# Mixed expert and attention network on one core: sums and low pieces taken out of the routing's way, the first tile's order, dummy products in PE's pauses, and a first attention batch prepared block by block

## The chip, the cores and the metric

The kernel runs on one core of one Trainium2 chip. The metric is the device time of one execution in microseconds. The engines are PE (TensorE), DVE (VectorE), ACT (ScalarE), POOL (GpSimd) and SP (SyncE, which here only issues transfers). Each works through its own queue in order, and they meet at semaphores.

## The reference, cut to what matters

```python
# x [8, 256, 512], cond [8, 512]
h  = gru(initial=cond, inputs=x)                    # 256 steps one after another
s  = einsum('bsd,ed->bse', h, w_gate_router)        # 8 experts
tv, ti = top_k(s, 2)
w  = sum(softmax(tv)[..., None] * one_hot(ti, 8), axis=-2)
hid = silu(gate_e(h)) * up_e(h)                     # 192 wide, per expert
x1 = x + einsum('bsef,edf,bse->bsd', hid, w_down, w)

scale, shift = split(cond @ W_emb + b_emb)
xn = rms_norm(x1, g_norm) * (1 + scale) + shift
q, k, v = split(xn @ W_qkv)                         # 16 heads of 32
q, k = rms_norm(q, g_q), rms_norm(k, g_k)
o  = softmax(q k^T / sqrt(32)) v
o2 = o + o @ W_out

t = lambda w: clip(round(w / (mean(abs(w)) + 1e-8)), -1, 1)
out = x1 + (sigmoid(o2 @ t(w1).T) * (o2 @ t(w2).T)) @ t(w3).T    # 1408 wide
```

## The kernel before

Everything is in one launch. Products are made in fp16 from a high part and a low part of each operand (`high_*` writes the high part, `low_*` the rest), three products for each exact one. Each stage is a list of calls per engine, written out by hand, and no scheduler changes the order. PE, DVE, ACT, POOL and SP each have a function in each of two blocks: the recurrence until about 825 us, and everything else.

The second block begins with the **routing**. For each of 16 groups of 128 tokens (`NG`), ACT and POOL split the states, PE multiplies them with the router and turns them (`route`), DVE sums the scores and takes the two largest (`sum_scores`, `top`, `top_index`), and ACT and DVE in turn copy the turned rows (`take_rows`), which SP saves to `hrows`. Between these stand pieces of weights: ACT makes their high part (`high_piece`), DVE their low part (`low_piece`), and SP loads the next piece into one of three buffers when the low part of the third before it is done. Pieces 8 to 15 are the experts' down weights, 16 to 19 those of q, k and v, 20 and 21 those of the output. Before its first sum DVE made the ternary thresholds and the adaptive scales (`thresholds`, `adapt`), which are used only much later.

Then come the **lists** that sort tokens by expert (`slots`, `owners`). DVE finds each token's slot, PE adds up ranks (`rank`), and 32 products of one-hot matrices (`rows_of_tiles`) give each tile of 128 slots its token rows. Their right side is `hot_row`: a one-hot tile number times the token's group offset. POOL then gathers the rows of each tile from `hrows` by indirect transfers into three buffers.

There are 39 **tiles** (`TILES`). For each, PE turns the rows (`turn_x`), DVE copies them (`take_x`), PE makes gate and up (`gate_up`), ACT and DVE the hidden values, PE turns these and multiplies them down, ACT scales the result, and POOL scatters it. `rest_of_tiles` gives the shares and is made once, beside the first tile.

**Attention** goes through eight batches of two blocks of 128 tokens. DVE or POOL add the two expert rows of a token (`first_sum`, `sum_rows`), DVE the residual; ACT makes the row norm (`square_rows`, `root_rows`, `unit_rows`), PE turns the rows (`turn_back`), and DVE (`adaptive`) or ACT (`turned`) apply scale and shift. PE makes six projections per batch (`project`: q and k of block 0, q and k of block 1, then v of each). Each q and k piece is copied, squared by POOL, summed, rooted, multiplied, split and stacked (`take_out`, `squares`, `sum_squares`, `root`, `invert`, `normalise_qk`, `high_qk`, `low_qk`, `stack`), and `scores` with `maximum` gives the row maxima of the 16 heads. In later batches this lies among the work of the batch before. For the first batch nothing else is there to do, and it stands by itself at the end of PE's, ACT's and DVE's functions: all of one step, then all of the next.

## Time and profile before

| | |
|---|---|
| Timed runs | 1696.36 us median of 3 (1693.38 to 1698.99) |
| Profiled execution | 1703.78 us, span 1702.0 us |
| Busy | PE 1552.9 us (91%), DVE 1187.9 (70%), ACT 900.0 (53%), POOL 609.9 (36%) |
| Recurrence | 0 to 825 us |
| Routing and lists | 825 to 869 us |
| 39 tiles | 869 to 1031.5 us |
| First batch prepared | 1038.7 to 1093.3 us |
| Eight batches and the ternary layers | to 1702 us |

Busy time is an average over stages with different limits, so each stage is read by itself. A row of the timeline gives the start, the duration, the engine and the line; the bracket at its end is how long the engine had been idle and what ended that. PEclk is the granted clock of PE as a part of 2.4 GHz. A duration of several merged instructions (x12) is the time from the first one's start to the last one's end.

### The profile page before, as it was taken

How to read it: one execution, taken by the hardware profiler on the slowest of the kernel's cores; microseconds unless marked ns; L12 is line 12 of the kernel's file. 1: busy time of each engine (PE TensorE's matmuls, PEld its weight loads, DVE VectorE, ACT ScalarE, POOL GpSimd, SP SyncE). 2: the span in 40 equal slices, each digit the busy share in tenths (PEclk: the TensorE clock that was granted, in tenths of full speed). 3: DMA queues.
4: the chain of work that ended last, by engine and by line, in shares of the span. 5: the costliest groups of instructions: out<-in, count | busy, mean ns of one | idle time of the engine just before them, and what ended most of it. 6: DMA issues, size and time to landing. Idle time of an engine off the chain costs nothing.

```text
span 1702.0 us, 76385 instructions
## 1 busy us (share of the span) xinstructions
PE 1552.9 (91%) x31935; PEld 1208.4 (71%) x31935; DVE 1187.9 (70%) x4289; ACT 900.0 (53%) x3329; POOL 609.9 (36%) x1819
## 2 busy tenths in 40 slices
PE   7999999999999999999759996778889888999999
PEld 6999999999999999999736553346556655544444
DVE  6778778787877778888865443677777777672231
ACT  6555555455555556655615444477777777531230
POOL 0333333333333333333625544344445443560000
PEclk9999999999999999955569997789999998999999
DMA  4110110101110011110435734000000010220001
GB/s 182 51 28 11 43 30 21 45 11 56 42 41 12 8 47 46 48 29 29 137 131 165 251 126 160 26 1 26 27 1 2 2 57 2 75 76 31 19 1 50
DMA packets 45735, 91.28 MB, mean 54 GB/s; under 512 B 6608, under 2 KB 25168, under 8 KB 45392
## 3 DMA queue, kind: packets, MB, share of 16 engines
q1 hardware_dynamic: 39152, 65.94, 12.0%
q0 software_dynamic: 6240, 20.45, 3.5%
q8 instruction: 254, 4.16, 1.0%
q14 instruction: 89, 0.73, 0.1%
HBM read 67.69 MB, written 18.61 MB: 51 GB/s over the span
## 4 chain that ended last, share of the span: by engine, by line
PE 29%; DVE 7%; ACT 7%; issue 3%; POOL 2%; DMA 1%; another core or an unknown queue 1%; SPq 0%; ACTq 0%; POOLq 0%; DVEq 0%
PE bank L1292 9%; PE bank L1178 5%; PE bank L1370 4%; PE bank L1102 3%; PE bank L1124 2%; ACT arena L1520 2%; POOL arena L2106 2%; ACT arena L1525 2%; PE bank L1196 1%; DVE arena L1917 1%; PE bank L1091 1%; PE bank L1249 1%; PE bank L1234 1%; PE bank L1273 1%
## 5 line engine op out<-in xcount | busy, mean ns | idle before, releaser
L412 PE MATMUL bank<-arena 128*128 128x8 f16 x12288 | 501.4, 170 | 9.2 <-issue 4.4
L415 PE MATMUL bank<-arena 128*128 128x16 f16 x12288 | 498.3, 182 | 3.4 <-issue 2.2
L412 PEld LDWEIGHTS bank<-arena 128*128 128x128 f16 x12288 | 412.7, 97 | 36.6 <-ACT bank L509 19.3
L415 PEld LDWEIGHTS bank<-arena 128*128 128x128 f16 x12288 | 412.8, 97 | 6.6 <-issue 5.0
L676 POOL TENSOR_TENSOR arena<-arena 128x16 f32<-128x16 f32 x512 | 116.8, 228 | 534.4 <-DVE arena L619 519.7
L479 ACT ACTIVATE arena<-arena 128x16 f32<-128x16 f32 x512 | 114.6, 224 | 308.6 <-DVE arena L598 308.3
L609 DVE TENSOR_TENSOR_SCAN arena<-arena,bank 128x64 f32<-128x64 f32 x512 | 146.8, 287 | 20.3 <-PE bank L415 3.1
L598 DVE TENSOR_REDUCE arena<-bank 128x16 f32<-128x48 f32 x512 | 100.2, 196 | 84.0 <-PE bank L415 78.7
L1292 PE MATMUL bank<-arena 128*128 128x512 f16 x704 | 153.6, 379 | 0.0
L385 PE MATMUL bank<-arena 128*128 128x256 f16 x1008 | 148.3, 273 | 2.6 <-issue 2.6
L1178 PE MATMUL bank<-arena 128*128 128x512 f16 x576 | 137.0, 389 | 4.0 <-DVE arena L1872 3.8
L615 DVE TENSOR_TENSOR_SCAN arena<-arena 128x48 f16<-128x48 f32 x512 | 134.1, 262 | 5.6 <-ACT arena L489 0.2
L489 ACT ACTIVATE arena<-arena 128x16 f32<-128x16 f32 x512 | 119.2, 233 | 24.1 <-DVE arena L609 6.1
L485 ACT ACTIVATE arena<-arena 128x16 f32<-128x16 f32 x512 | 110.3, 215 | 36.2 <-DVE arena L603 3.3
L1292 PEld LDWEIGHTS bank<-arena 128*128 128x128 f16 x704 | 68.9, 98 | 81.2
L603 DVE TENSOR_REDUCE arena<-bank 128x16 f32<-128x48 f32 x512 | 106.1, 207 | 27.1 <-PE bank L415 2.4
L2106 POOL TENSOR_TENSOR arena<-arena 128x512 f16<-128x512 f32 x56 | 67.7, 1210 | 147.3 <-ACT arena L1525 147.2
L677 POOL COPY arena<-arena 128x16 f32<-128x16 f32 x512 | 118.3, 231 | 0.0
L619 DVE TENSOR_TENSOR_SCAN arena<-arena 128x48 f32<-128x48 f32 x512 | 117.2, 229 | 0.4
L624 DVE TENSOR_TENSOR arena<-arena 128x16 f16<-128x16 f32 x512 | 95.8, 187 | 17.7
L1178 PEld LDWEIGHTS bank<-arena 128*128 128x128 f16 x576 | 56.8, 99 | 66.1 <-issue 5.6
L678 POOL COPY arena<-arena 128x16 f32<-128x16 f32 x512 | 102.6, 200 | 0.0
(209 smaller groups left out, 2676.8 us busy)
## 6 DMA issues: line engine op xcount, KB each, us to landing
arena<-yrows SPq DMA_DIRECT2D x16, 512.0 KB, 4.2
arena<-in_wgu SPq DMA_DIRECT2D x48, 128.0 KB
arena<-in_wdn SPq DMA_DIRECT2D x8, 512.0 KB
hrows<-arena SPq DMA_DIRECT2D x16, 256.0 KB, 4.5
arena<-in_xtok SPq DMA_DIRECT2D x16, 256.0 KB
out_y<-arena SPq DMA_DIRECT2D x16, 256.0 KB, 2.0
arena<-in_wih SPq DMA_DIRECT2D x4, 768.0 KB, 7.5
arena<-in_whh SPq DMA_DIRECT2D x4, 768.0 KB, 11.5
```

Of the source, the lines that this page charges most:

```text
L385: mm = nc.tensor.matmul(bank[7][:, half_of(mt)], wihs[:, wp, k, mt, :], xs[:, xp, k, half_of(c)], start=(i % 24 == 0), stop=(i % 12 == 11) ...
L412: mm = nc.tensor.matmul(dst[:, j * B:(j + 1) * B, 1], w, h[:, 0], start=home not in opened, stop=False, skip_group_check=True)
L415: mm = nc.tensor.matmul(dst[:, j * B:(j + 1) * B, 1:3], w, h.rearrange("p a c -> p c a"), start=home not in opened, stop=False, skip_group ...
L479: A.activation(fn[:, HALF[g], 3], rzp[:, 0, HALF[g]], ACT.Sigmoid, scale=1 / SWX).then_inc(r_act[g], 1)
L489: A.activation(inh[:, HALF[g], 0], sn[:, HALF[g], 3], ACT.Tanh, scale=1 / SWX).then_inc(n_act[g], 1)
L609: V.tensor_tensor_scan(flat(sn[:, HALF[g]]), flat(fn[:, HALF[g]]), flat(gate_sums(t, 2, g)), 0.0, ALU.mult, ALU.add).then_inc(n_pre[g], 1)
L615: V.tensor_tensor_scan(flat(mv[:, t % 2, 0, HALF[g]]), flat(fh[:, HALF[g]]), flat(inh[:, HALF[g]]), 0.0, ALU.mult, ALU.add).then_inc(h_hi[ ...
L619: V.tensor_tensor_scan(flat(sh[:, HALF[g]]), flat(fh[:, HALF[g]]), flat(inh[:, HALF[g]]), 0.0, ALU.mult, ALU.add).then_inc(h_f32[g], 1)
L676: G.tensor_tensor(inh[:, HALF[g], 1], zeros[:, :], sh[:, HALF[g], 2], ALU.subtract)
L677: G.tensor_copy(inh[:, HALF[g], 2], sh[:, HALF[g], 2])
L1178: mm = nc.tensor.matmul(bank[5 + i % 2][:, :], xn[:, x_, k, half * P:(half + 1) * P], wqs[:, w_, k, col:col + D], start=(n == 0), stop=(n ...
L1292: mm = nc.tensor.matmul(up_bank(a, u), w12[:, mt, a, k, :], o2p[:, 2 * c:2 * c + 2, part, k, :], start=(part == 0 and k == 0), stop=(part ...
```

## The change

It has five parts.

1. `thresholds` and `adapt` are divided. DVE reads their sums out of the banks where it did before (`sum_thresholds`, `take_adapt`); the rest follows after tiles 6 and 10.
2. DVE's low parts of pieces 14 and 15 go from the routing to behind the first tile's copy. The copy of the last group's rows goes behind the operation that PE's ranking waits for. SP's loads follow: that of piece 17 came before the last saved rows, now after them, and 17 and 18 wait for the two moved parts.
3. `hot_row` is made by ACT in 16 scaled copies, one for each group, instead of one product on DVE. PE's first and third eight products wait for eight of them, its second and fourth for all.
4. PE does ten dummy products of 512 columns (`keep_warm`, into a bank that is overwritten later) while the first gather is on its way, and the first tile's product before the second tile's turn. The wait for the last low piece goes from there to the first tile's down product.
5. The first batch is prepared block by block and piece by piece. Two further runs of dummy products, nine and seven, stand around the first two turns. Block 0 is scaled by DVE and ACT together, split and projected before block 1 is ready; q and k pieces have a root and a reciprocal each; blocks 2 and 3 (batch 1) are scaled by ACT instead of DVE, after the first stacks; and only the first stack comes before the scores, the others between them. For that, `turn_bank` gives the first four blocks banks of their own.

```diff
 def row_bank(g):
...
-def turn_bank(g):
+def turn_bank(g, k=0):
...
+    if g < EARLY:
+        return bank[((4, 4, 2, 2), (7, 7, 7, 7), (2, 2, 2, 2), (3, 3, 3, 3))[g][k]]
...
 NORM_X_AT = {9: 0, 10: 1}
+STACK_Q = {1: 1, 5: 2, 9: 3}
+STACK_K = {2: 1, 6: 2, 10: 3}
...
             save_rows(g)
-            if g % 2 == 0 and g > 0:
+            if g % 2 == 0 and 0 < g < NG - 2:
...
                 load_piece(sp, n)
-        for n in range(NGU + 2 + NG // 2, PIECES):
+        for n in range(NGU + 1 + NG // 2, PIECES):
...
         def rows_of_tiles():
...
-            pe.wait_ge(slot_step, SLOT_STEPS["row hot"])
...
                     pe.wait_ge(low_hot, i // 8 + 1)
+                    pe.wait_ge(probs, 1 + g + 8)
...
+        def keep_warm(n, moving):
...
+            for i in range(n):
+                nc.tensor.matmul(bank[3][:, :], id1[:, :], moving, start=True, stop=True)
...
                 pe.wait_ge(goal_step, GOALS["goal"])
+            else:
+                pe.wait_ge(pw_lo, split_count(NEXP - 1))
...
         rows_of_tiles()
+        keep_warm(10, hot_low[:, 0, 0:4, :].rearrange("p g t -> p (g t)"))
         pe.wait_ge(row_step, ROW_STEPS["owners"])
-        pe.wait_ge(pw_lo, split_count(NEXP - 1))
...
         turn_x(0)
-        turn_x(1)
...
             if i == 0:
+                turn_x(1)
         def turn_back(g):
...
             if g >= 2:
-                pe.wait_ge(xnf_done, g - 1)
+                pe.wait_ge(xnf_done, g)
             for k in range(KT):
-                mm = nc.tensor.transpose(turn_bank(g)[:, k * P:(k + 1) * P],
+                mm = nc.tensor.transpose(turn_bank(g, k)[:, k * P:(k + 1) * P],
...
         def project(b, i, first=False):
...
-            if i == 0:
+            if i == 0 and not first:
                 pe.wait_ge(xn_lo, KT * (b + 1))
+            elif i in (0, 2) and first:
...
+                pe.wait_ge(xn_lo, KT // 2 * (i // 2 + 1))
...
-        def stack(b, g):
...
-            for a, done, mms in ((0, qs_done, qs_mm), (1, ks_done, ks_mm)):
+        def stack(b, g, which=(0, 1)):
...
+            for a in which:
+                done, mms = (qs_done, ks_done)[a], (qs_mm, ks_mm)[a]
...
                 if h in OUT_AT and len(turned_in(b)) > 0:
-                    pe.wait_ge(xnf_done, EARLY + 2 * b + 1 + OUT_AT[h])
+                    pe.wait_ge(xnf_done, EARLY + 2 * b + 2 + OUT_AT[h])
...
+        pe.wait_ge(yb_in[0], 16)
+        keep_warm(9, wqs[:, 0, 0, 0:D])
...
         turn_back(1)
+        keep_warm(7, wqs[:, 0, 0, 0:D])
         project(0, 0, True)
+        project(0, 1, True)
         turn_back(2)
-        project(0, 1, True)
+        project(0, 2, True)
         turn_back(3)
-        for i in range(2, 6):
+        for i in range(3, 6):
             project(0, i, True)
-        for g in range(4):
-            stack(0, g)
-        pe.wait_ge(xnf_done, EARLY)
+        stack(0, 0)
         for h in range(H):
+            if h in STACK_Q:
+                stack(0, STACK_Q[h], (0,))
+            if h in STACK_K:
+                stack(0, STACK_K[h], (1,))
...
+        pe.wait_ge(xnf_done, EARLY + 1)
...
         A.activation(pr[:, :, :], dif[:, :, :], ACT.Sigmoid, scale=1 / SWX).then_inc(probs, 1)
+        act.wait_ge(slot_step, SLOT_STEPS["tile hot"])
+        for g in range(NG):
+            A.activation(hot_row[:, :, g, :], hot_tile[:, :, g, :], ACT.Copy, scale=token[:, g:g + 1])\
+                .then_inc(probs, 1)
...
             act.wait_ge(turn_mm, g + 1)
-            for k in range(KT):
-                op = A.activation(xnf[:, b, k, half * P:(half + 1) * P], turn_bank(g)[:, k * P:(k + 1) * P],
+            for k in range(2 if g == 0 else 0, KT):
+                op = A.activation(xnf[:, b, k, half * P:(half + 1) * P], turn_bank(g, k)[:, k * P:(k + 1) * P],
...
+        def high_tile(g):
...
+            act.wait_ge(xnf_done, g + 2)
+            A.activation(xn[:, 0, :, g * P:(g + 1) * P], xnf[:, 0, :, g * P:(g + 1) * P], ACT.Copy)\
+                .then_inc(xn_hi, 1)
...
         def norm_x(b, half):
-            act.wait_ge(xnf_done, 2 * b + 2)
+            act.wait_ge(xnf_done, 2 * b + 3)
         def root(b):
...
             A.activation(rmsk[:, :, :], ssk[:, :, :], ACT.Sqrt, scale=1 / DH, bias=epsb[:, :])\
+                .then_inc(rmsk_done, 1)
...
+        def first_root(i):
...
+            act.wait_ge(ssk_done, i + 1)
+            A.activation(rmsk[:, i, :], ssk[:, i, :], ACT.Sqrt, scale=1 / DH, bias=epsb[:, :])\
...
         unit_rows(1)
+        turned(0)
+        high_tile(0)
         turned(1)
-        norm_x(0, 0)
-        norm_x(0, 1)
+        high_tile(1)
...
         unit_rows(2)
+        take_out(0, 0)
+        square_rows(4)
+        root_rows(4)
         unit_rows(3)
-        take_out(0, 0)
         take_out(0, 1)
-        for g in (4, 5):
-            square_rows(g)
-            root_rows(g)
+        first_root(0)
+        square_rows(5)
+        root_rows(5)
+        high_qk(0, 0)
         take_out(0, 2)
+        first_root(1)
+        high_qk(0, 1)
         take_out(0, 3)
-        root(0)
+        first_root(2)
         take_out(0, 4)
+        high_qk(0, 2)
+        first_root(3)
+        high_qk(0, 3)
         take_out(0, 5)
-        for n in range(4):
-            high_qk(0, n)
+        stack(0, 0)
+        stack(0, 1)
+        turned(2)
+        stack(0, 2)
+        turned(3)
+        stack(0, 3)
...
         norm_x(1, 1)
-        for g in range(4):
-            stack(0, g)
...
             V.tensor_tensor(both[:, :, :], picked[:, 0], picked[:, 1], ALU.add).then_inc(slot_step, 1)
+            take_rows(NG - 1)
...
                             ALU.is_equal).then_inc(slot_step, 1)
-            dve.wait_ge(slot_step, SLOT_STEPS["tile hot"])
-            V.tensor_tensor(hot_row[:, :, :, :], hot_tile[:, :, :, :],
-                            token.unsqueeze(1).unsqueeze(3).broadcast_to((P, 2, NG, TILES)),
-                            ALU.mult).then_inc(slot_step, 1)
...
-        def adapt():
+        def take_adapt():
...
+        def adapt():
...
             if g < NG:
-                if g % 2 == 1:
+                if g % 2 == 1 and g < NG - 1:
                     take_rows(g)
-                elif g > 0:
+                elif 0 < g < NG - 2:
                     low_piece(NGU + g // 2 - 1)
-        low_piece(NEXP - 1)
...
         rest_hot()
-        dve.wait_ge(probs, 1)
         take_x(0)
+        low_piece(NEXP - 2)
+        low_piece(NEXP - 1)
...
             low_hidden(i)
+            if i == 6:
+                thresholds()
+            elif i == 10:
+                adapt()
         def adaptive(g):
...
             dve.wait_ge(turn_mm, g + 1)
-            for k in range(KT):
+            for k in range(KT if g > 0 else 2):
...
-        def norm_x(b):
-            for half in range(2):
-                dve.wait_ge(xn_hi, 2 * b + half + 1)
-                V.tensor_tensor(xn_half(1, half), xnf_half(b, half), xn_half(0, half),
-                                ALU.subtract).then_inc(xn_lo, KT // 2)
+        def norm_x(g):
+            dve.wait_ge(xn_hi, g + 1)
+            V.tensor_tensor(xn[:, 1, :, g * P:(g + 1) * P], xnf[:, 0, :, g * P:(g + 1) * P],
+                            xn[:, 0, :, g * P:(g + 1) * P], ALU.subtract).then_inc(xn_lo, KT // 2)
...
         def sum_squares(b, i):
...
         def invert(b):
-            dve.wait_ge(rmsk_done, b + 1)
+            dve.wait_ge(rmsk_done, b + 4)
             V.reciprocal(rk[:, :, :], rmsk[:, :, :]).then_inc(rk_done, 1)
-            dve.wait_ge(rk_done, b + 1)
+            dve.wait_ge(rk_done, b + 4)
...
+        def first_invert(i):
...
+            dve.wait_ge(rmsk_done, i + 1)
+            V.reciprocal(rk[:, i, :], rmsk[:, i, :]).then_inc(rk_done, 1)
+            dve.wait_ge(rk_done, i + 1)
...
         adaptive(0)
+        norm_x(0)
         residual(2)
-        norm_x(0)
+        norm_x(1)
         residual(3)
-        for g in (2, 3):
-            invert_rows(g)
-        for g in (2, 3):
-            adaptive(g)
+        invert_rows(2)
+        residual(4)
+        invert_rows(3)
+        residual(5)
         sum_squares(0, 0)
-        residual(4)
+        invert_rows(4)
+        first_invert(0)
+        normalise_qk(0, 0)
         sum_squares(0, 1)
-        residual(5)
-        invert_rows(4)
+        low_qk(0, 0)
         invert_rows(5)
+        first_invert(1)
+        normalise_qk(0, 1)
         sum_squares(0, 2)
+        low_qk(0, 1)
+        first_invert(2)
+        normalise_qk(0, 2)
         sum_squares(0, 3)
-        invert(0)
-        for i in range(4):
-            normalise_qk(0, i)
-        for n in range(4):
-            low_qk(0, n)
-        for g in range(4):
-            stack(0, g)
+        low_qk(0, 2)
+        first_invert(3)
+        normalise_qk(0, 3)
+        low_qk(0, 3)
+        stack(0, 0)
         for h in range(H):
+            if h in STACK_K:
+                stack(0, STACK_K[h])
```

Three places in the instruction order show what moved. The first is DVE's queue from its last score sum to the operation after PE's ranking (`TENSOR_REDUCE` is the sum, `SCALAR_TENSOR_TENSOR` of 1024 a low piece, `COPY` the row copy). Before:

```order
L1661 TENSOR_REDUCE arena<-bank 128x8 [waits score_mm]
L1666 MAX arena<-arena 128x8 [waits scores_sum]
L1670 MAX_INDEX arena<-arena 128x8 [waits top8]
L1657 COPY arena<-bank 128x1024 [waits xrow_out3,rows_mm]
L1666 MAX arena<-arena 128x8 [waits scores_sum]
L1670 MAX_INDEX arena<-arena 128x8 [waits top8] x2
L1641 SCALAR_TENSOR_TENSOR arena<-arena 128x1024 [waits pw_hi]
L1674 TENSOR_TENSOR arena<-arena 128x16 x2
```

And in the changed kernel:

```order
L1711 TENSOR_REDUCE arena<-bank 128x8 [waits score_mm]
L1716 MAX arena<-arena 128x8 [waits scores_sum]
L1720 MAX_INDEX arena<-arena 128x8 [waits top8]
L1716 MAX arena<-arena 128x8 [waits scores_sum]
L1720 MAX_INDEX arena<-arena 128x8 [waits top8] x2
L1724 TENSOR_TENSOR arena<-arena 128x16 x2
L1726 CAST arena<-arena 128x32 [waits top_ix]
L1729 TENSOR_TENSOR arena<-cst,arena 128x128 [waits slot_step]
L1729 TENSOR_TENSOR arena<-cst,arena 128x128
L1733 TENSOR_TENSOR arena<-arena 128x128 [waits slot_step]
L1707 COPY arena<-bank 128x1024 [waits xrow_out3,rows_mm]
L1737 TENSOR_TENSOR arena<-bank,cst 128x128 [waits route_mm]
```

The row copy and the low piece no longer stand between the last sum and the lists.

The second is PE's queue from the last list products (128x39) to the first tile's product. Before:

```order
L1072 MATMUL bank<-arena 128x39 x7
L1091 MATMUL bank<-id,arena 128x128 [waits xg_in0,pw_lo,row_step]
L1091 MATMUL bank<-id,arena 128x128 x7
L1091 MATMUL bank<-id,arena 128x128 [waits xg_in1]
L1091 MATMUL bank<-id,arena 128x128 x7
L1143 TENSOR_LOAD arena
```

And now:

```order
L1077 MATMUL bank<-arena 128x39 x7
L1094 MATMUL bank<-arena,id 128x512 x10
L1101 MATMUL bank<-id,arena 128x128 [waits xg_in0,row_step]
L1101 MATMUL bank<-id,arena 128x128 x7
L1154 TENSOR_LOAD arena
```

Ten products are new, and the second tile's turn is behind the first tile's product.

The third is PE's queue from the first turns of attention rows. Before:

```order
L1159 MATMUL bank<-cst,arena 128x128 [waits unit_done]
L1159 MATMUL bank<-cst,arena 128x128 x3
L1178 MATMUL bank<-arena 128x512 [waits xn_lo]
L1178 MATMUL bank<-arena 128x512 x11
L1159 MATMUL bank<-cst,arena 128x128 [waits xnf_done,unit_done]
```

And now:

```order
L1094 MATMUL bank<-arena,id 128x512 [waits yb_in0]
L1094 MATMUL bank<-arena,id 128x512 x8
L1171 MATMUL bank<-cst,arena 128x128 [waits unit_done]
L1171 MATMUL bank<-cst,arena 128x128 x3
L1171 MATMUL bank<-cst,arena 128x128 [waits unit_done]
L1171 MATMUL bank<-cst,arena 128x128 x3
L1094 MATMUL bank<-arena,id 128x512 x7
L1193 MATMUL bank<-arena 128x512 [waits xn_lo]
L1193 MATMUL bank<-arena 128x512 x23
```

Dummy products stand on both sides of the turns, and two projections follow each other where there was one.

## Rows read from the trace of the kernel before

**Rows 1.** Stretches of the run: busy us per engine (x instructions), PEclk, DMA share, GB/s.
```profile
882.40:1031.50 149.10, 141.19 (x1059) 85.59 (x1056) 74.00 (x208) 72.87 (x159) 76.55 (x72) 1.00 0.50 167
...
1038.70:1093.30 54.60, 35.80 (x185) 17.98 (x186) 33.07 (x65) 22.10 (x45) 18.47 (x16) 0.72 0.24 83
```

**Rows 2.** Timeline at the routing's start: start us, us, engine line, op, [idle <-releaser].
```profile
826.03 1.07 DVE L1796 TENSOR_SCALAR gam<-gam 128x3 f32<-128x3 f32 x1
...
831.88 0.36 PE L1038 MATMUL bank<-wrs,arena 128*128 128x16 f16 x8 [2.37 <-DVE arena L1661]
...
833.14 1.02 ACT L1402 ACTIVATE arena<-bank 128x1024 f16<-128x1024 f16 x1 [1.66 <-PE bank L1051]
```

**Rows 3.** Timeline between the last route and the lists.
```profile
850.90 0.38 PE L1038 MATMUL bank<-wrs,arena 128*128 128x16 f16 x8 [0.84 <-POOL arena L2061]
...
850.94 1.20 DVE L1641 SCALAR_TENSOR_TENSOR arena<-arena 128x1024 f16<-128x1024 f32 x1
...
852.40 0.69 DVE L1657 COPY arena<-bank 128x1024 f16<-128x1024 f16 x1
...
853.36 1.20 DVE L1641 SCALAR_TENSOR_TENSOR arena<-arena 128x1024 f16<-128x1024 f32 x1
...
854.48 0.28 DVE L1674 TENSOR_TENSOR arena<-arena 128x16 f32<-128x16 f32 x2
```

**Rows 4.** Timeline of the lists: token rows, the shares' sigmoid, comparisons.
```profile
861.74 1.46 DVE L1717 TENSOR_TENSOR arena<-arena,cst 128x1248 f16<-128x1248 f16 x1
...
854.79 0.23 ACT L1442 ACTIVATE arena<-arena 128x32 f32<-128x32 f32 x1 [2.07 <-DVE arena L1674]
...
863.44 4.62 DVE L1726 TENSOR_TENSOR arena<-cst,arena 128x1024 f16<-128x1024 f32 x4
```

**Rows 5.** Timeline of PE at the first two tiles.
```profile
873.20 1.01 PE L1091 MATMUL bank<-id,arena 128*128 128x128 f16 x8 [4.63 <-DMA arena<-hrows,arena]
...
875.15 1.03 PE L1091 MATMUL bank<-id,arena 128*128 128x128 f16 x8 [0.93 <-DMA arena<-hrows,arena]
...
876.15 4.02 PE L1102 MATMUL bank<-arena 128*128 x12
...
882.37 1.95 PE L1102 MATMUL bank<-arena 128*128 x11
```

**Rows 6.** Timeline of PE where the first batch is prepared.
```profile
1043.23 1.97 PE L1159 MATMUL bank<-cst,arena 128*128 128x128 f32 x8 [11.75 <-ACT arena L1470]
...
1048.96 5.30 PE L1178 MATMUL bank<-arena 128*128 128x512 f16 x12 [3.76 <-DVE arena L1872]
...
1057.77 5.34 PE L1178 MATMUL bank<-arena 128*128 128x512 f16 x24
...
1074.24 4.68 PE L1196 MATMUL bank<-id,arena 128*96 128x128 f16 x40 [5.54 <-DVE arena L1896]
...
1093.31 5.32 PE L1178 MATMUL bank<-arena 128*128 128x512 f16 x12
```

**Rows 7.** Groups by line, 1038.7 to 1093.3: busy us, mean ns | idle, releasers.
```profile
L1906 DVE TENSOR_REDUCE arena<-bank 128x2 f32<-128x512 f32 x16 | 10.2, 687 | 1.5 <-PE bank L1215 1.2
...
L2111 POOL TENSOR_TENSOR arena<-arena 128x256 f16<-128x256 f32 x4 | 4.4, 1120 | 5.5 <-ACT arena L1484 5.5
...
L1478 ACT ACTIVATE arena<-bank,ada 128x128 f32<-128x128 f32 x4 | 1.5, 455 | 1.4 <-PE bank L1159 1.4
...
L1484 ACT ACTIVATE arena<-arena 128x512 f16<-128x512 f32 x4 | 2.3, 616 | 0.0
```

**Rows 8.** Timeline: a late gather, and DVE beside POOL.
```profile
847.73 2.11 DVE L1641 SCALAR_TENSOR_TENSOR arena<-arena 128x1024 f16<-128x1024 f32 x1
...
870.58 2.23 POOL L2065 DMA_INDIRECT arena<-hrows,arena  x1 [0.30 <-issue]
...
935.54 0.97 POOL L2065 DMA_INDIRECT arena<-hrows,arena  x1 [0.30 <-issue]
...
943.39 0.62 PE L1091 MATMUL bank<-id,arena 128*128 128x128 f16 x8 [3.00 <-issue]
```

More of the change, by code:

```diff
@@ L1794, in thresholds @@
                                     AX.XY, ALU.add).then_inc(prep, 1)
+                def thresholds():
                     dve.wait_ge(prep, 1)
```

8 lines of the change are left out of this document (4 added, 4 removed).

## The prediction

> **What bounds the kernel now.** I read the stretches first. From 882.40 to 1031.50, the 39 expert tiles, PE is busy 141 of 149 us at full clock. From 1038.70 to 1093.30, where the first batch of attention is prepared, it is busy 35.8 of 54.6 us at a mean granted clock of 0.72 [rows 1]. So the tiles are PE's, and the preparation is a chain of handovers that an order can shorten. Then I read the timeline around four places, for the wait that ends last there. Where the routing starts, PE's third turn waits 2.37 us for DVE's first sum, and ACT then waits 1.66 us [rows 2]. Where the lists start, three DVE copies stand in front of them [rows 3]. At the first tile PE runs at the lower clock: twelve products take 4.02 us, against 1.95 for eleven a tile later [rows 5]. In the preparation the first projection's twelve products take 5.30 us, later ones 2.67 (5.34 for 24); PE waits 5.54 us for the last normalised piece, and the next batch's projection starts at 1093.31 [rows 6]. With the clock column, 0.44 us a product is the 1.2 GHz level and 0.22 us the 2.4 GHz one.
>
> **Part 1, sums before the thresholds.** DVE did nine small operations before its first sum, four of them at 1.03 to 1.15 us (one is shown) [rows 2]. Two remain, 0.2 us each. DVE is then ready at about 826.3, and PE's third turn can go when its second ends, at 829.5 (831.88 - 2.37). The gain that is passed on is ACT's wait of 1.66 us, because ACT's copies feed POOL, and POOL's last split is what PE's last turn waits for [rows 3]. I take 1.7.
>
> **Part 2, the lists.** PE's last score ends at 851.28 (850.90 + 0.38); the lists' first operation starts at 854.48 [rows 3]. Between them stood a low piece that held DVE until 852.1 (850.94 + 1.20), a row copy of 0.69 and a low piece of 1.20. All three go. Their successors: the row copy lies under PE's ranking, the low pieces behind the first tile's copy. What is left between score and lists is the sum, two maxima and three index operations, 0.8 us. So the lists start at 851.28 - 1.7 + 0.8 = 850.4: 4.1 us gained by parts 1 and 2. Bounds: 2.4, if the start is held elsewhere, to 4.8, if PE's whole 2.37 comes through.
>
> **Part 3, token rows by ACT.** DVE's product of 1.46 us [rows 4] goes. ACT makes 16 scaled copies of 78 elements instead, while DVE compares. No row shows that operation. A row of 32 elements takes 0.23 us [rows 4], so 16 take 3.7 and hide under the four comparisons of 4.62 us: 1.46 gained. The scaled copies out of a bank come every 0.375 us (1.50 for four) [rows 7]; then the sixteenth lands after 6.0 us, 24 of PE's products wait for it, and the lists end 0.6 us later than before. The shape is nearer the 32-element row, but not free: I take 1.2 gained, bounds +1.5 and -0.6.
>
> **Part 4, first tile.** Ten dummy products fill PE's wait of 4.63 us for the gather (10 x 0.44 = 4.4, so they end before the rows land), and the first tile's product comes before the second's turn [rows 5]. Between the landing at 873.20 and the second tile's product at 882.37 PE did 9.17 us. The order alone gains nothing: a copy of 1024 elements, 0.69 us as in rows 3, now stands between first turn and product, where 0.93 us of waiting for the second gather goes. The clock does: at 2.4 GHz it is turn 0.6, copy 0.7, product 2.1, turn 0.6, shares 2.1, turn 0.6 and 0.2 of handovers, 6.9. I take 2.3 gained; bounds 0 (clock as before) and 2.5.
>
> The low pieces now run on DVE in this stretch and free two piece loads (768 KB each) that SP formerly issued before the gathers. When 16 blocks of 256 KB were loaded at once, a gather issued at 935.54 cost PE one wait of 3.00 us [rows 8]. Here it is 1.5 MB against 4, the tile hit is the third or fourth, and the turn is 8 us away. I take 0.5 lost, bounds 0 and 4.
>
> DVE's low piece took 2.11 us beside POOL's subtraction [rows 8] and 1.20 alone [rows 3]; a gather's issue took 2.23 beside DVE's two-input product [rows 8]. The Trainium skill (SBUF — State Buffer, Who interferes with whom) says that a DVE instruction with two SBUF inputs contends with a GpSimd one that reads SBUF, and infers that writing descriptors is not hit. By it the moved low pieces delay no gather and the sum stays; by the 2.23 row one gather is issued 1.3 us later, which is inside the bound of 4.
>
> **Part 5, thresholds and scales among tiles 6 and 10.** DVE is busy 74 of 149 us there [rows 1], 1.9 us free a tile. Nothing lost; uncovered, it would be 1 us or two.
>
> **Part 6, preparing the first batch**, measured from the landing of the first expert rows at 1038.7.
> (a) Nine dummy products, 4.0 us, end at 1042.7, before the first turn at 1043.23 [rows 6]. The first block is now turned, scaled and split alone: half of the turns (1.0), two scalings on ACT and two on DVE at once (0.75), one copy 0.62 and one subtraction 0.7, with 0.2 of handovers [rows 7]. The first projection starts at 1046.5 instead of 1048.96.
> (b) PE has then been busy since 1038.7 but for half a microsecond. Before, all twelve products of the first projection ran low and the following ones did not [rows 6]. I expect it up before 1046.5: the first projection takes 2.65 instead of 5.30. Together 5.1 us, and the sixth projection ends at 1063.6 instead of 1068.7.
> (c) Before, all four pieces were normalised after one common root, and PE waited 5.54 us. Now piece 3 is finished beside projections 5 and 6. By the passes of like size in rows 7 its chain is, estimated, two on ACT at 0.62, one on POOL at 1.1, three on DVE at 0.69, and 0.8 for root, reciprocal and a short copy: 5.2, against 5.3 for two projections. ACT also carries squares, roots and unit rows there, 1.9 us more by my count. Stacks start at 1065.5 instead of 1074.24.
> (d) Before, four stacks and 16 maxima took 18.9 us (1074.24 to 1093.14). Now one stack (2.4, of four in about 9) is followed by 16 maxima at 0.687 and three DVE copies at 0.69 [rows 7], 13.1 us and 0.2: the last maximum is at 1081.2.
> (e) The next late thing: ACT splits batch 1's rows only after the last stack copy, about 1078.3, and POOL needs 4.4 us for its four low parts [rows 7]. Before, they lay under the stacks. The next projection starts at 1083.0, not 1081.4.
> So it starts 10.3 us sooner. Bounds: 6.0 if the clock stays low in (b), where seven more dummies at 0.44 us also hold the first projection to 1048.2; 13 if (e) vanishes and that projection runs at full clock, 2.65 instead of 5.32.
>
> **Sum.** -4.1 - 1.2 - 2.3 + 0.5 - 10.3 = -17.4 us on the profiled execution's 1703.78 (span 1702.0 and 1.8 around it): 1686.4. That execution is 7.4 us over the median of the timed runs, 1696.36, which the new time will be compared with: 1679.0.
>
> **Rivals.**
> B, the clock rises late. For: before, PE did a whole projection at the low level each time (1048.96 and 1093.31) [rows 6], and no dummy run is shown; turns and short products leave gaps. Against: both dummy blocks join work that follows within a microsecond. Price: part 4 gives 0, part 6 gives 6.0: -4.1 - 1.2 + 0.5 - 6.0 = -10.8, 1685.6. The Trainium skill (TensorE: Matmul & The Clock Gate, Part 1) says the default is the throttled state and that the number of slow products differs from run to run; by it B could be true of some runs only, giving a median between 1679 and 1685.6.
> C, the lists come no sooner, so that this part doesn't do what it says. For: row saves and loads crowd the stretch before them, and gathers need every save. Against: the lists need no transfer. Price 5.3: 1684.3.
> D, ACT sets the pace of part 6, since takes, roots, squares and high parts of six blocks now stand in one queue in front of each other. Price: (c) and (d) give 5.3 less, so 1684.3. Against: ACT was busy 22.1 of 54.6 us [rows 1].
> E, slower: late gathers become the rule. The moved loads push the first gathers behind, and with three buffers a gather late by 3.00 us, as the one at 935.54 [rows 8], slows each of three tiles by 1.0; over 39 tiles that is 39.0 against the 17.4, 1718. It decides from 0.45 us per tile on (17.4 / 39). Against: nothing refills the lag once the loads have ended, and the one late gather cost its 3 us once.
> F, better: (e) vanishes, full clock in the next projection, 5 us more: 1674.
>
> **How the numbers follow.** Forecast 0.52 (its own range 1675 to 1684), B 0.16, C 0.10, D 0.10, E 0.05, F 0.07. The range 1672 to 1688 takes in all but E and the tails. About 0.3%, 5.1 us, is what a measurement here tells from no change: everything but E is faster by more, less 0.05 for two of B, C and D coming together. Faster 0.90, same 0.05, slower 0.05.
>
> **What would show it.** The lists' first operation 25.3 us after the routing's first product rather than 29.4; PE's rows before the first gather full of 512-column products; first expert product in 2.1 us rather than 4.0; first projection in 2.7 us; the span from first sum of expert rows to batch 1's projection 44 us instead of 54.6; still about 149 us for the 39 tiles. Wrong would be a granted clock of 0.5 there, PE waiting for gathers at tiles 2 to 5, or a new ACT wait in front of the stacks.

## The result, and the profile after

The changed kernel takes 1677.8 us, the median of five runs (1671.18 to 1680.19), against 1696.36 (1689.39 to 1699.68); the ratio is 0.9896, 95% interval 0.9871 to 0.9920. 1679.0 was forecast. Timed again on another chip the ratio was 0.9921 (0.9898 to 0.9943), 1682.11 against 1696.84.

The two profiled executions lie further apart than the medians, 1669.3 against 1702.0 us of span, so they must not be compared as a whole. This table cuts each at the same events. "Lists" and "rows" are the starts of the first sorting operation and of the tiles' finished token rows, both from the routing's first product. "Second product" is that of the second tile, from the token rows on. "Tiles" goes from there to the first sum of expert rows, "preparation" from that sum to batch 1's projection, and "rest" from there to the end. `again` are repeats on another chip.

| us | before | changed | before again | changed again |
|---|---|---|---|---|
| Recurrence | 825.12 | 817.12 | 833.41 | 826.66 |
| Lists | 29.36 | 25.65 | 30.87 | 25.66 |
| Rows | 43.49 | 38.26 | 44.98 | 38.26 |
| Second product | 13.76 | 10.67 | 13.15 | 12.30 |
| Tiles | 156.36 | 150.17 | 151.77 | 155.29 |
| Preparation | 54.58 | 43.99 | 53.21 | 45.84 |
| Rest | 608.69 | 609.09 | 610.58 | 610.35 |

Of the 32.7 us between the spans, 8.0 are the recurrence and 6.2 the tiles. The tiles are 3.5 us longer in the changed kernel in the repeats, so their 6.2 us are not shown to be the change's. The edit doesn't touch the recurrence, but that was the shorter one with the change both times, by 8.0 and 6.8 us; whether this is chance stays open. The other stages give 5.23 + 3.09 + 10.59, less 0.40 of the rest: 18.5 us, against 18.6 between the medians. The same sum over the repeats is 15.2 us, and the medians on the other chip lie 14.7 apart, so the medians need no share of the recurrence.

Two stretches of the changed kernel (busy us of PE, PE's weight loads, DVE, ACT, POOL, then PEclk, DMA share, GB/s) answer to [rows 1]:

```profile
866.05:1016.20 150.15, 139.94 (x1059) 86.12 (x1056) 74.47 (x216) 76.49 (x162) 80.06 (x76) 0.99 0.53 182
1016.20:1060.20 44.00, 34.50 (x201) 18.81 (x202) 32.68 (x58) 26.03 (x58) 16.40 (x15) 0.88 0.27 102
```

The first row reaches to the first sum of expert rows; PE's last product of the tiles ends at 1008.9, 142.9 us after the row's start, where it took 149.1 before. PE's busy time among the tiles is nearly the same. The seven small operations of DVE now made there take 1.3 us of it together, and the tiles took 150.2 to 155.4 us with them and 151.8 to 156.4 without, so no cost stands out. In the preparation the same work fits into 44.0 us, at a clock of 0.88 instead of 0.72.

The timeline from the last score to the first tile's product answers to [rows 3 to 5]:

```profile
842.12 0.17 DVE L1711 TENSOR_REDUCE arena<-bank 128x8 f32<-128x16 f32 x1 [0.30 <-PE bank L1043]
...
842.77 0.26 DVE L1724 TENSOR_TENSOR arena<-arena 128x16 f32<-128x16 f32 x2
...
850.01 4.11 ACT L1468 ACTIVATE arena<-arena,cst 128x78 f16<-128x78 f16 x16 [6.20 <-DVE arena L1763]
...
850.21 4.62 DVE L1773 TENSOR_TENSOR arena<-cst,arena 128x1024 f16<-128x1024 f32 x4
...
854.27 1.07 PE L1077 MATMUL bank<-arena 128*128 128x39 f16 x24 [1.57 <-ACT arena L1468]
...
855.17 4.25 PE L1094 MATMUL bank<-arena,id 128*128 128x512 f16 x10
...
857.31 2.81 DVE L1783 TENSOR_TENSOR arena<-arena 128x1248 f16<-128x1248 f16 x2
857.35 2.23 POOL L2134 DMA_INDIRECT arena<-hrows,arena  x1 [0.30 <-issue]
...
859.98 0.61 PE L1101 MATMUL bank<-id,arena 128*128 128x128 f16 x8 [0.56 <-DMA arena<-hrows,arena]
860.63 0.69 DVE L1821 COPY arena<-bank 128x1024 f16<-128x1024 f16 x1 [0.50 <-PE bank L1101]
861.24 2.40 DVE L1691 SCALAR_TENSOR_TENSOR arena<-arena 128x1024 f16<-128x1024 f32 x2
861.25 0.95 POOL L2134 DMA_INDIRECT arena<-hrows,arena  x1 [0.30 <-issue]
861.47 2.12 PE L1112 MATMUL bank<-arena 128*128 x12 [0.88 <-DVE arena L1821]
```

DVE starts the lists 0.65 us after the last sum begins. Sixteen scaled copies on ACT take 4.11 us and lie beside the comparisons. The first product takes 2.12 us at the higher clock level, where it took 4.02. The moved low pieces follow the first tile's copy, and a gather's issue that begins together with the first of them takes 0.95 us.

PE in the preparation (same columns), which answers to [rows 6]:

```profile
1020.72 1.27 PE L1171 MATMUL bank<-cst,arena 128*128 128x128 f32 x8 [0.75 <-ACT arena L1497]
1021.82 1.67 PE L1094 MATMUL bank<-arena,id 128*128 128x512 f16 x7
1023.73 5.35 PE L1193 MATMUL bank<-arena 128*128 128x512 f16 x24 [0.23 <-DVE arena L1928]
...
1043.64 1.94 PE L1212 MATMUL bank<-id,arena 128*96 128x128 f16 x16 [3.32 <-DVE arena L1958]
1046.78 0.59 PE L1231 MATMUL bank<-arena 96*128 96x256 f16 x2 [1.20 <-ACT arena L1542]
...
1060.21 4.44 PE L1193 MATMUL bank<-arena 128*128 128x512 f16 x12
```

Two projections take 5.35 us, each the forecast 2.67. PE waits 3.32 us for the stacks' input, 2.2 less than before, and the next projection follows the turned maxima at once. Three groups of the same stretch (busy, mean ns | idle, releaser) answer to [rows 7]:

```profile
L1968 DVE TENSOR_REDUCE arena<-bank 128x2 f32<-128x512 f32 x16 | 10.3, 687 | 2.5 <-PE bank L1231 2.5
L1950 DVE SCALAR_TENSOR_TENSOR arena<-arena 128x512 f32<-128x512 f32 x4 | 4.6, 1142 | 0.2
L2180 POOL TENSOR_TENSOR arena<-arena 128x256 f16<-128x256 f32 x4 | 2.5, 664 | 18.1 <-ACT arena L1517 18.1
```

### The profile page after: what moved, and what is told of

Same layout as the page of the kernel before. It is cut to its first block, busy times and chain, and to the rows that moved or that the text cites. A ratio compares the mean times of both kernels' runs of the same rounds, so it can differ in the third digit from the quotient of the medians.

```text
span 1669.3 us, 76463 instructions
## 1 busy us (share of the span) xinstructions
PE 1548.3 (93%) x31961; PEld 1206.1 (72%) x31961; DVE 1182.9 (71%) x4281; ACT 908.3 (54%) x3358; POOL 607.7 (36%) x1819
## 4 chain that ended last, share of the span: by engine, by line
PE 31%; ACT 7%; DVE 5%; POOL 4%; issue 2%; DMA 1%; SPq 0%; ACTq 0%; POOLq 0%; DVEq 0%
PE bank L1308 9%; PE bank L1393 5%; PE bank L1193 4%; PE bank L1112 4%; PE bank L1136 2%; POOL arena L2175 2%; ACT arena L1559 2%; ACT arena L1564 2%; POOL arena L2130 1%; PE bank L1212 1%; PE bank L1289 1%; DVE arena L1979 1%; PE bank L1101 1%; PE bank L1265 1%; PE bank L1250 1%
## 6 DMA issues: line engine op xcount, KB each, us to landing
arena<-in_whh SPq DMA_DIRECT2D x4, 768.0 KB, 10.6
```

## The experiments

Medians of different calls stand on different chips (before: 1705.25, 1694.20 and 1696.84 us), so only ratios and stages are compared across them. Six runs have one time each (before_again 1708.86, after_again 1690.51, old_turns 1675.14, hot_dve 1674.45, old_turns_warm 1679.19, pieces_front 1684.62 us); single times scatter by more than what these runs ask for, so only their stages are used.

### One half of the change at a time

`front_only` is the kernel before with parts 1 to 4 (in the forecast's numbering 1 to 5); `prep_only` is the kernel before with the new preparation alone. In short, against the changed kernel:

```diff
 # front_only
...
-                keep_warm(9, wqs[:, 0, 0, 0:D])
-                stack(0, 0)
+                for g in range(4):
+                    stack(0, g)
...
 # prep_only
-                keep_warm(10, hot_low[:, 0, 0:4, :].rearrange("p g t -> p (g t)"))
+                thresholds()
+                adapt()
+                low_piece(NEXP - 1)
...
```

> The kernel before with every part of the change but the last: sums before thresholds, lists sooner, token rows by ACT, ten dummy products and the new order at the first tile; the first batch prepared as before. Theory (parts add up): token rows 38.3 us after the routing's start (43.5 before), second tile's product 48.9 us after it (57.3), preparation 54.6 us, time 8.3 us under the kernel before, 1688.0. Rival (tiles made shorter by the change): tiles 150 us and 14.5 us under the kernel before, 1681.9.

> The kernel before with only the last part of the change: the first attention batch prepared block by block, with its nine and seven dummy products; routing, lists and first tile as before. Theory (the parts add up, and only the stages that they touch move): preparation 44.0 us as in the changed kernel against 54.6 before, routing to token rows 43.5 us and second tile's product 57.3 us after the routing's start as before, tiles 156 us, time 10.6 us under the kernel before, 1685.8. Rival (the 6.2 us by which the tiles were shorter in the changed kernel's profile come from the change): they stay near 156 us here and near 150 us in the kernel with the other parts alone.

> The kernel before once more, for how its stages scatter from one execution to the next. Theory (recurrence and tiles scatter by themselves): the recurrence between 817 and 826 us and the 39 tiles between 149 and 157 us, while routing, lists and preparation repeat within 0.3 us. Rival (the tiles are shorter by the change): tiles 156 us again.

> The changed kernel once more. Theory (scatter): tiles somewhere from 149 to 157 us, recurrence from 817 to 826; lists 25.3, token rows 38.3, second tile 48.9 us after the routing's start, preparation 44.0 us, each within 0.3. Rival: tiles 150 us again.

Measured: front_only has the ratio 0.9944 (0.9923 to 0.9964), prep_only 0.9938 (0.9910 to 0.9966). Their product is 0.9882, and the changed kernel had 0.9896 and 0.9921: within the intervals the halves add up. Stages: front_only has lists 25.66, rows 38.26, second product 12.22, preparation 54.53; prep_only has 30.40, 44.51, 13.61 and 45.69. Each moves only its own beyond what the kernel before scatters by. Tiles took 155.42 and 153.21 us, so a shortening of the tiles by the front half falls.

The start of the lists scatters in the old order only: 29.36, 30.87 and 30.40 us, against 25.64 to 25.67 in all ten profiles with the whole new front. In the two late ones a row copy of DVE waited for the save of earlier rows, 2.00 us in before again and 1.38 in prep_only:

```profile
857.21 0.69 DVE L1657 COPY arena<-bank 128x1024 f16<-128x1024 f16 x1 [2.00 <-DMA hrows<-arena]
```

### Without the dummy products

```diff
-                keep_warm(10, hot_low[:, 0, 0:4, :].rearrange("p g t -> p (g t)"))
...
-                keep_warm(9, wqs[:, 0, 0, 0:D])
...
-                keep_warm(7, wqs[:, 0, 0, 0:D])
```

> All three blocks of multiplications without a use (ten before the first tile's turn, nine and seven in the preparation) are gone. Theory (the forecast's): they give the clock and nothing else. The first projection is back at 5.3 us instead of 2.7 (before's row), part of the 24 projections behind it still runs at 0.50 of the clock, so the preparation takes 47.5 to 50 us instead of 44 to 46, the first tile's second product comes 12.5 to 13.5 us after the rows of the tiles instead of 10.7 to 12.3: 5 us more than the change, ratio to before 0.992. Rival (they are beside the wait for the recurrence's stacks, which DVE and ACT set): preparation within 1 us of the change's, ratio 0.989.

Ratio 0.9900 (0.9872 to 0.9927), 1678.93 against 1694.20 us: the loss of 5 us didn't come, and the interval overlaps the changed kernel's. In the whole time the worth of the changed kernel's dummies is therefore not shown; the stages show it. The preparation took 47.05 us, 1.2 to 3.1 over the changed kernel's, and the second product 12.81 us. PE in the preparation of no_warm:

```profile
1026.27 1.94 PE L1170 MATMUL bank<-cst,arena 128*128 128x128 f32 x8 [11.90 <-ACT arena L1494]
1029.72 7.79 PE L1192 MATMUL bank<-arena 128*128 128x512 f16 x24 [1.51 <-DVE arena L1925]
...
1050.76 1.09 PE L1211 MATMUL bank<-id,arena 128*96 128x128 f16 x16 [2.02 <-DVE arena L1955]
```

The clock did come late: 24 products took 7.79 us and not 5.35, and they began 0.52 us later after the first sum. But of these 3.0 us, 1.3 came out of the wait before the stacks (2.02 instead of 3.32), so the stacks start only 1.65 us later. The block-by-block order alone brings most of the gain: 47.05 us against 54.58 and 53.21 in the two profiles of before.

### Order and dummies at the first tile

```diff
 # old_turns
                 turn_x(0)
+                turn_x(1)
...
-                        turn_x(1)
 # old_turns_warm: that, and
-                keep_warm(10, hot_low[:, 0, 0:4, :].rearrange("p g t -> p (g t)"))
+                keep_warm(12, hot_low[:, 0, 0:4, :].rearrange("p g t -> p (g t)"))
...
                 turn_x(0)
+                keep_warm(6, hot_low[:, 0, 0:4, :].rearrange("p g t -> p (g t)"))
+                turn_x(1)
```

> The second tile's turn is ahead of the first tile's product again, the rest of the change stays. Theory: the first product waits for the second gather and its turn, 0.6 to 1.5 us later after the rows of the tiles (7.0 to 7.6 instead of 6.1 us), and the second product comes no later than in the change, since the turn only changes its place: 10.7 to 12.3 us. Rival (the swap itself makes the gain of the first tiles): the second product comes at 13.2 to 13.8 us as in the kernel before.

> The second tile's turn stands ahead of the first product, and the time for which it waits for the second gather, 1.43 us, is filled with six multiplications without a use (and 12 instead of 10 before the first turn). Theory: most of what the old order cost beside the change, 2.8 us at the second product, is the clock, lost in that wait: the first product takes 2.1 instead of 3.77 us, the second comes 11.7 to 11.8 us after the rows of the tiles instead of 13.43. Rival (the order itself costs it): 13.0 to 13.4 us.

PE in old_turns, and then in old_turns_warm:

```profile
859.56 0.61 PE L1101 MATMUL bank<-id,arena 128*128 128x128 f16 x8 [0.39 <-DMA arena<-hrows,arena]
861.60 0.62 PE L1101 MATMUL bank<-id,arena 128*128 128x128 f16 x8 [1.43 <-DMA arena<-hrows,arena]
862.60 3.77 PE L1112 MATMUL bank<-arena 128*128 x12 [0.38 <-issue]
```

```profile
861.38 0.61 PE L1101 MATMUL bank<-id,arena 128*128 128x128 f16 x8 [0.88 <-DMA arena<-hrows,arena]
861.82 1.46 PE L1094 MATMUL bank<-arena,id 128*128 128x512 f16 x6
863.16 0.62 PE L1101 MATMUL bank<-id,arena 128*128 128x128 f16 x8
864.16 2.12 PE L1112 MATMUL bank<-arena 128*128 x12 [0.38 <-issue]
```

In old_turns both turns run at the higher level (0.61), but between them PE waits 1.43 us for the second gather, the one whose issue takes 2.23 us, and the product runs slowly. With the wait filled the product takes 2.12 us. The second product comes after (each value is one profile):

| us after the rows | no dummies | ten dummies | pauses filled too |
|---|---|---|---|
| Both turns first | 13.76, 13.15, 13.61 | 13.43 | 11.80 |
| First product first | 12.81 | 10.67, 10.69, 11.01, 12.22, 12.30, 12.33 | 11.14, 10.69 |

Neither alone is worth much beside the three readings of the old state. The theory holds for the clock's share, 1.63 us (13.43 to 11.80); the order gives another 1.1 us at full clock (11.80 to 10.69), which neither theory had.

The changed order has two kinds of execution. This is changed again, PE and then the granted clock in steps of 2 us:

```profile
864.71 3.70 PE L1094 MATMUL bank<-arena,id 128*128 128x512 f16 x10
869.53 0.61 PE L1101 MATMUL bank<-id,arena 128*128 128x128 f16 x8 [1.12 <-DMA arena<-hrows,arena]
871.02 3.74 PE L1112 MATMUL bank<-arena 128*128 x12 [0.89 <-DVE arena L1821]
```

```profile
866.00:868.00 2.00, 2.00 (x7) 0.76 (x6) 1.97 (x5) 0.00 (x0) 1.70 (x2) 0.62 0.31 76
868.00:870.00 2.00, 0.88 (x10) 0.46 (x8) 1.66 (x2) 0.00 (x0) 1.70 (x2) 1.00 0.26 72
870.00:872.00 2.00, 1.11 (x7) 0.55 (x5) 1.83 (x3) 0.00 (x0) 1.43 (x2) 0.74 0.66 186
872.00:874.00 2.00, 2.00 (x8) 0.96 (x7) 1.18 (x2) 0.00 (x0) 0.00 (x0) 0.50 0.81 228
```

The clock rose during the dummies, was full in the turn, and fell again after PE had been idle 1.12 us for the gather and 0.89 us for the copy. The product then took 3.74 us. Where it rose later, so that ten dummies took 4.25 us and the idle time before the turn was 0.56 us, it stayed up.

### Token rows back on DVE

```diff
-                            pe.wait_ge(probs, 1 + g + 8)
...
+                    V.tensor_tensor(hot_row[:, :, :, :], hot_tile[:, :, :, :],
+                                    token.unsqueeze(1).unsqueeze(3).broadcast_to((P, 2, NG, TILES)),
+                                    ALU.mult).then_inc(slot_step, 1)
```

> The product of token numbers with the slots' one-hot rows is back on DVE as one operation, the rest of the change stays. Theory: before's row has it at some 4 us on DVE, against 16 copies of 0.26 us on ACT beside which DVE goes on; the rows of the tiles come 39.6 to 39.8 us after the routing's start instead of 38.26. Rival (ACT's copies only move the wait, PE waits for them as it waited for DVE): 38.3 us.

The rows came at 39.77 us: the move to ACT is worth 1.5 us, all of the DVE product of 1.46 [rows 4]. (The "some 4 us" given there for that product was wrong; the range expected was not.) The rival falls.

### Low pieces in front of the lists again

```diff
+                low_piece(NEXP - 2)
+                low_piece(NEXP - 1)
                 slots()
...
-                low_piece(NEXP - 2)
-                low_piece(NEXP - 1)
```

> DVE's low parts of pieces 14 and 15 stand directly in front of the lists again, the rest of the change stays. Theory (the forecast's 2.4 us of 4.1): the lists start 28.05 us after the routing instead of 25.65. Rival (they fit into DVE's idle time before the last score, as the first of them nearly did): 26.9 us, and the rest of the measured 3.7 is by the thresholds.

The lists came at 27.90 us, 2.25 later than in the changed kernel; the two pieces stand there as one row:

```profile
846.55 2.34 DVE L1691 SCALAR_TENSOR_TENSOR arena<-arena 128x1024 f16<-128x1024 f32 x2
848.81 0.28 DVE L1724 TENSOR_TENSOR arena<-arena 128x16 f32<-128x16 f32 x2
```

So 2.25 of the 3.71 us are the pieces, and 1.46 are left for the thresholds and the row copy. That remainder is a difference; the thresholds were not put back alone. The rows divide it: the last route starts 24.58 us after the routing's first product instead of 25.78 [rows 3], 1.20 us, and 0.26 are won behind it. Against the two other profiles of the old order the lists come 4.7 and 5.2 us sooner.

### The pauses filled

hold_clock has 14 dummies before the first turn, three between it and the product, and 14 ahead of the first stack. hold_on has, against the changed kernel:

```diff
-                keep_warm(10, hot_low[:, 0, 0:4, :].rearrange("p g t -> p (g t)"))
+                keep_warm(12, hot_low[:, 0, 0:4, :].rearrange("p g t -> p (g t)"))
...
                 turn_x(0)
+                keep_warm(3, hot_low[:, 0, 0:4, :].rearrange("p g t -> p (g t)"))
...
+                for i in range(14):
+                    nc.tensor.matmul(bank[1][:, :], id1[:, :], wqs[:, 0, 0, 0:D], start=True, stop=True)
                 stack(0, 0)
...
+                    for i in range((h > 8) + (h > 12)):
+                        nc.tensor.matmul(bank[1][:, :], id1[:, :], wqs[:, 0, 0, 0:D], start=True, stop=True)
                     scores(0, h, True)
+                for i in range(3):
+                    nc.tensor.matmul(bank[1][:, :], id1[:, :], wqs[:, 0, 0, 0:D], start=True, stop=True)
```

> Multiplications without a use are added where PE still stood still in the changed kernel: 14 instead of 10 ahead of the first tile's turn, 3 between the turn and the first product, 14 ahead of the first stack, where PE waited 3.3 us. Theory: the pauses of about 1 us after the warming are what lost the clock again in the run with 12.3 us to the second product; filled, every run has 10.7 us (1.6 us less), and the stacks' turns take 0.6 instead of 1.06 us each, the preparation 42 to 44 us; in all 2 to 3 us less than the change, ratio 0.987 to before. Rival (the stretch goes by ACT's and DVE's copies): the second product comes sooner, the preparation stays at 44 to 46 us, ratio 0.989. A second rival: the dummies come late and stand in front of the stack: each 0.2 to 0.4 us, up to 3 us more.

> As the run with the pauses filled, with 12 instead of 14 multiplications without a use ahead of the first turn (14 ended 0.45 us too late), and with eleven more between the last seven scores and four ahead of the turned maxima, where PE stood still and the granted clock fell before batch 1's projection. Theory (the clock goes with pauses): that projection takes 2.7 instead of 5.25 us, and the first scores of the second kind come 2.5 us sooner after it, unless the row that they read has not landed; the first tile's second product comes 10.7 us after the rows of the tiles instead of 11.14. Together 2 to 3 us less than 42.5 + 5.1 from the first sum of expert rows to those scores, ratio to before 0.986. Rival: the dummies push each score by 0.2 us, since PE's copy partner DVE is what the scores wait for, and the gain is given back: ratio 0.988 to 0.989.

> The changed kernel, once more on the same chip as the run beside it, for its ratio to before and for the spread of its stages. If the dummies in the pauses are worth what their stages showed (1 us at the tile beside one reading of the change, 0 to 1.6 beside the others; 1.5 to 3.4 us in the preparation), this one comes out 2 to 5 us above it. Rival: within 1 us of it.

(hold_on has ten dummies between the scores and three ahead of the turned maxima, not the eleven and four named.) hold_clock: ratio 0.9873 (0.9847 to 0.9900). hold_on: 0.9860 (0.9839 to 0.9882), 1672.49 us, beside the changed kernel's 1682.11 and 0.9921 (0.9898 to 0.9943) on the same chip. The intervals don't touch, so hold_on beats both kernels.

In both profiles the clock stayed up from the first turn to the first product, against three of six with the pauses open; two profiles give no rate.

The stages, from the first sum of expert rows, where the last column is the first of the scores made for the values:

| us | first stack | turned maxima | batch 1's projection | those scores |
|---|---|---|---|---|
| changed | 27.42 | 43.86 | 43.99 | 48.26 |
| changed, timed | 27.71 | 45.51 | 45.68 | 50.16 |
| changed again | 27.86 | 45.67 | 45.84 | 50.52 |
| no_warm | 29.07 | 46.88 | 47.05 | 51.37 |
| hold_clock | 27.41 | 42.31 | 42.47 | 47.56 |
| hold_on | 27.44 | 42.51 | 42.64 | 46.35 |

From the first stack to the maxima the windows of changed again and of hold_on are:

```profile
1060.37:1078.20 17.83, 14.15 (x97) 10.04 (x97) 13.05 (x20) 7.88 (x14) 3.12 (x5) 0.55 0.00 1
```

```profile
1043.28:1058.35 15.07, 11.10 (x109) 7.67 (x110) 12.71 (x20) 7.88 (x14) 3.18 (x5) 1.00 0.01 1
```

At 0.55 of the clock PE is busy for 14.15 of 17.83 us; at full clock the stretch takes 15.07, of which DVE is busy 12.71. The end of it, in hold_clock and then in hold_on:

```profile
1061.82 0.37 PE L1238 MATMUL bank<-cst,arena 128*32 128x128 f32 x1 [0.88 <-DVE arena L1971]
1061.98 5.25 PE L1194 MATMUL bank<-arena 128*128 128x512 f16 x12
1067.07 0.60 PE L1251 MATMUL bank<-arena 97*128 97x256 f16 x4
```

```profile
1058.48 2.75 PE L1194 MATMUL bank<-arena 128*128 128x512 f16 x12
1062.19 0.61 PE L1251 MATMUL bank<-arena 97*128 97x256 f16 x4 [0.97 <-DMA arena<-arena]
```

The projection takes 2.75 instead of 5.25 us, as expected, but only 1.2 us arrive: the scores now wait 0.97 us for the row of maxima, which comes by DMA. That was the condition in the expectation.

hold_on's stages give 0.3 us at the second product and 3.8 to those scores, 4.1 beside the changed kernel timed with it. Their medians differ by 9.6. In the two profiles the recurrence, which the edit doesn't touch, differs by 5.2; what the rest of the 9.6 is in the timed runs stays open, and I claim only the 4.

## Why the prediction was right

The mechanisms that carry the sum were seen, but that 18.6 us stand beside the forecast 17.4 is partly luck: the other chip gave 14.7, the sum over the repeats 15.2, and several terms below miss in opposite directions.

**Lists (forecast 4.1, measured 3.7, and 4.7 to 5.2 against the late profiles).** DVE was free in time and PE's third route went without a wait. The pieces were sized 2.4 and measured 2.25; the start was sized 1.7, and the last route starts 1.20 us sooner. That row saves crowd the old order, as rival C says, is true, but it adds to the gain; the rival itself falls.

**Token rows by ACT (1.2, measured 1.5).** The unshown operation takes 0.26 us each, between the two rows and next to the nearer one.

**First tile (2.3 gained, 0.5 lost; measured 0.8 to 3.1, nothing lost that the rows show).** The sum was right, its reason only in part. "The order alone gains nothing" failed: the order gives 0.3 to 1.0 us without dummies (12.81 against 13.15 to 13.76) and 1.1 at full clock, because the second gather's landing is no longer awaited before the first product, which starts 6.1 to 6.6 us after the rows instead of 7.5 to 7.7. And the clock gained by dummies is not kept for certain. The forecast counted PE as busy from the dummies to the product and left out the two pauses between them. Loads and gathers did not collide: PE waited for no gather at tiles 2 to 5, and rival E falls.

What delays a gather's issue is the order in which it and DVE begin. Beside DVE's 128x1248 product of two inputs it took 2.23 us in all 14 profiles (the product itself is not among [rows 8]; it is in the timeline after). Beside the low pieces it took 0.95 us where both began within 0.02 us, in five profiles of which the changed kernel's is one, but 1.99 in front_only, 1.53 in old_turns and 1.74 in old_turns_warm, where a piece was already running. In front_only:

```profile
870.18 2.35 DVE L1652 SCALAR_TENSOR_TENSOR arena<-arena 128x1024 f16<-128x1024 f32 x2
870.23 1.99 POOL L2083 DMA_INDIRECT arena<-hrows,arena  x1 [0.30 <-issue]
```

The Trainium skill (SBUF — State Buffer, Who interferes with whom) infers that writing descriptors is not hit by DVE's second SBUF input. These issues were hit, so the measurement decides against it. The forecast's alternative, one gather issued 1.3 us later, thus came true in part, by 0.6 to 1.1 us in three of the runs, and PE waited at none of the tiles 2 to 5 for it.

**Thresholds among the tiles (0; measured nothing beyond the tiles' scatter of 6 us).**

**Preparation (10.3, measured 10.6 in the profile; 7.4 between the two repeats and 8.8 between front_only and prep_only).** Step by step, forecast and then measured from the first sum, in the changed kernel's own profile: first projection 7.8 and 7.51; its products 2.65 and 2.67; stacks 26.8 and 27.42; from there to the turned maxima 15.7 and 16.44, at a clock of 0.80 in this profile and 17.8 at 0.55 in the repeat. The stacks were forecast from the last piece's chain, but DVE worked from 1031.7 to 1042.0 almost without a pause, and L1950 took 1.14 us in the mean and not 0.69; for the last piece it took 0.69. That its queue over all four pieces is the bound is read from the rows, not tried. Step (e), 1.8 us with POOL's low parts and a handover, did not occur: the parts took 0.66 us each instead of 1.12 and were done before the maxima. Two terms too small by 1.4 and one too large by 1.7 cancel. Where the clock was lost in the stacks the stage took 45.5 to 45.9 us (five of the eight profiles with this preparation unaltered). In before again the clock rose within the first projection, which took 4.07 us instead of 5.30; this and the loss in the changed kernel's repeat are why the repeats lie 7.4 apart. The forecast's upper bound of 13 leaves one of its two terms out: 10.3, 1.8 for (e) and 2.7 for the projection make 14.8, and by the same terms F's 5 us are 4.5.

The clock's price was too high: 10.3 with the clock up in the first projection and 6.0 with it low, behind dummies that then hold the projection back, set it at 4.3 us. That case never came; without the dummies it measured 1.2 to 3.1. A microsecond saved on a product in front of a wait mostly lengthens the wait.

**Rivals.** B, the clock late, is true in another form: it rose in time in every profile with the dummies and was lost later, at the first product in three of the six with the change's tile order and ten dummies. The Trainium skill (TensorE: Matmul & The Clock Gate, Part 1) says that the number of slow products differs from run to run; 2.12 against 3.74 us for the same twelve agrees. Its price was 1.6 us at the tile (12.30 to 10.67) and 1.9 in the preparation (45.84 to 43.99), not 6.6. D, ACT as the bound, is seen only as 1.20 us before the first scores. F came in half: (e) vanished, the projection stayed slow.

## What to carry to other kernels

Cut both executions at the same events before explaining a difference: here 14 of 33 us lay in the recurrence and the tiles, which scatter by as much from profile to profile. Price a faster piece of work by what waits behind it, not by its own duration. If dummy work is to raise the clock, fill every pause up to the work that needs it, and end it before what it stands in front of: fourteen where twelve fit cost 0.45 us. Look at what a gather's issue stands beside: DVE's product lengthened that of the second gather by 1.3 us in every profile, and in the old order PE waited for that gather.

## What the runs showed of the hardware that was not expected

- POOL's issue of a gather for the tiles mostly takes 0.94 to 0.97 us, the first one 1.17. Where it began while a DVE operation on two SBUF inputs (128x1248 or 128x1024) had been running for 0.04 us or more, it ended 0.81 to 0.83 us after that operation, 31 times in 14 profiles; where both began within 0.02 us, it took 0.95 at most.
- The granted clock was lost again after PE's pauses of 1.12 and 0.89 us, and after one of 1.43 us, shortly after it had risen; it was kept over 0.56 and 0.88 us in the changed kernel's profile.
- ACT's scaled copy of 128x78 in fp16 took 0.26 us, against 0.23 for 32 elements in fp32.
- POOL's subtraction of 256 elements took 0.66 us beside DVE's maxima out of a bank and 1.12 in the kernel before beside DVE's stacks and low parts. That the SBUF input of DVE makes the difference is argued, not tried.
- The same recurrence code took 814.65 to 833.41 us in 14 profiles.
